# Moving a layer norm's statistics behind the projections of the group before it, in an eight-core attention and feed-forward kernel

## The reference, cut to what matters

```python
def layernorm(x):  # over the last axis, 1024 wide
    return (x - mean(x)) / sqrt(var(x) + 1e-5)

# x: (4, 4096, 1024) f32
def attention(x):              # H = 1024, one head
    y = einsum('bsh,oh->bso', x, W_qkv).reshape(*x.shape, 3)
    q, k, v = y[..., 0], y[..., 1], y[..., 2]
    attn = softmax(einsum('bqh,bkh->bqk', q, k) / sqrt(1024))
    return einsum('bsh,oh->bso', einsum('bqk,bkh->bqh', attn, v), W_out)

def ffn(x):                    # F = 4096
    # router: 8 experts, top 2, the two weights normalised, then summed
    return (gelu(x @ w1 + b1) @ w2 + b2) * combine_sum

x = x + layernorm(attention(layernorm(x)))
x = x + layernorm(ffn(layernorm(x)))
```

## Time and profile before

| | |
|---|---|
| the two timed runs | 1795.23 and 1933.11 us; their median 1864.17 us |
| the profiled execution's own time | 1799.36 us |
| its span on the slowest core (core 0) | 1797.8 us |
| spans of all eight cores | 1783.2 to 1797.8 us |
| busy share of the span: TensorE, VectorE, ScalarE, GpSimd | 80%, 29%, 32%, 10% |

### The profile page before, as it was taken

How to read it: one execution, slowest core, us unless ns; L and a number is a source line. 1 busy time by engine, 2 the same in 40 slices (tenths; PEclk the granted TensorE clock), 3 DMA queues, 4 the chain that set the end, 5 groups by cost and what they waited for, 6 DMA issues and landing times.

```text
span 1797.8 us, 19351 instructions; the slowest of 8 cores (1783.2 to 1797.8 us)
## 1 busy us (share of the span) xinstructions
PE 1439.1 (80%) x6686; PEld 652.7 (36%) x6816; DVE 523.4 (29%) x1038; ACT 574.8 (32%) x1197; POOL 170.8 (10%) x149
## 2 busy tenths in 40 slices
PE   0477787778788888888888888864998898898896
PEld 0233333333344344444443333322343343343342
DVE  0443443554233333333333333322201201202100
ACT  0412111221022333333333333344354354354334
POOL 1000000000000000000000000112013013012003
PEclk9989999998988888888888888886899899999898
DMA  9312012110220101110110000869603003002002
GB/s 140 66 30 47 27 24 44 24 24 1 35 53 7 30 30 30 30 30 30 30 30 30 30 30 30 115 131 166 103 24 94 1 24 84 11 18 77 1 1 83
DMA packets 51617, 81.55 MB, mean 45 GB/s; under 512 B 19648, under 2 KB 27840, under 8 KB 51520
## 3 DMA queue, kind: packets, MB, share of 16 engines
q0 software_dynamic: 27280, 50.35, 16.6%
q1 hardware_dynamic: 24240, 29.94, 5.3%
HBM read 97.08 MB, written 20.97 MB: 66 GB/s over the span
## 4 chain that ended last, share of the span: by engine, by line
PE 70%; DVE 11%; issue 8%; DMA 5%; ACT 4%; POOL 1%; DVEq 0%; ACTq 0%; POOLq 0%; SPq 0%
PE pAll L185 36%; PE pAll L160 31%; DMA xgb<-xo 3%; PE pAll L216 3%; DVE ptb L751 2%; DMA qs<-qstage 2%; DVE vt L497 2%; DVE xfg L440 2%; DVE m L678 1%; DVE sm L375 1%; ACT diagb L731 1%; DVE qstage L468 1%; ACT pbuf L689 1%; DMA x2lt<-x2s 1%; PE pAll L1062 1%
## 5 line engine op out<-in xcount | busy, mean ns | idle before, releaser
L160 PE MATMUL pAll<-kf,qtile 128*128 128x512 bf16 x1000 | 252.1, 407 | 16.9 <-ACT pbuf L689 9.7
L160 PE MATMUL pAll<-x2f,w1b 128*128 128x512 bf16 x1002 | 240.6, 402 | 22.7 <-ACT h1g L1163 17.0
L185 PE MATMUL pAll<-vt,ptb 128*128 128x512 bf16 x1000 | 223.7, 382 | 2.4 <-DVE ptb L751 0.9
L185 PE MATMUL pAll<-w2b,h1g 128*128 128x512 bf16 x1002 | 220.2, 379 | 5.6 <-ACT h1g L1163 4.6
L678 DVE TENSOR_REDUCE m<-pAll 128x1 f32<-128x512 f32 x128 | 88.5, 692 | 330.2 <-PE pAll L160 328.8
L689 ACT ACTIVATE pbuf<-pAll,nb 128x512 bf16<-128x512 f32 x128 | 87.3, 683 | 241.3 <-DVE nb L683 241.3
L160 PEld LDWEIGHTS pAll<-kf,qtile 128*128 128x128 bf16 x1024 | 105.7, 105 | 154.3 <-issue 56.2
L160 PEld LDWEIGHTS pAll<-x2f,w1b 128*128 128x128 bf16 x1024 | 103.9, 102 | 157.1 <-issue 55.2
L185 PEld LDWEIGHTS pAll<-vt,ptb 128*128 128x128 bf16 x1024 | 100.8, 99 | 123.7 <-issue 4.7
L185 PEld LDWEIGHTS pAll<-w2b,h1g 128*128 128x128 bf16 x1024 | 99.9, 98 | 125.9 <-issue 6.0
L185 PE MATMUL pAll<-wvb,xfg 128*128 128x512 bf16 x504 | 115.2, 379 | 35.9 <-DVE vt L497 35.5
(11 more groups left out here) (109 smaller groups left out, 1094.6 us busy)
## 6 DMA issues: line engine op xcount, KB each, us to landing
xrt<-xo POOLq DMA_DIRECT2D x16, 512.0 KB, 6.3
x2s<-x2t SPq DMA_DIRECT2D x16, 512.0 KB, 3.3
w1b<-w POOLq DMA_DIRECT2D x8, 1024.0 KB, 32.8
w2b<-w POOLq DMA_DIRECT2D x4, 2048.0 KB, 43.6
x2rt<-x2s SPq DMA_DIRECT2D x16, 512.0 KB, 4.4
y<-yt SPq DMA_DIRECT2D x16, 512.0 KB, 2.9
xgb<-xo POOLq DMA_DIRECT2D x16, 256.0 KB, 7.4
qs<-qstage POOLq DMA_DIRECT2D x16, 256.0 KB, 2.8
```

The costliest lines, as they stand in the source:

```text
L160: return e.matmul(o(), l(), r(), start=st, stop=sp)
L185: return e.matmul(o(), l(), r(), start=st, stop=sp)
```

## The change: the loads stay ahead of the projections, the statistics go behind them

`emit_ln_group` is cut in two. `emit_ln_loads(g)` issues the four loads and is called where `emit_ln_group(g)` was. `emit_ln_stats(g)` holds everything else (sums, squares, the small instructions and the application to `xng`) and is called after the projections of group g-1, just ahead of the transposes of group g. No instruction is added or taken away.

```diff
-    def emit_ln_group(g):
-        p4 = (g % 2) * 4
-        fence_s, fence_v = ln4_war[g % 2]
+    ln_dma = {}
+
+    def emit_ln_loads(g):
         src_x = xo if g < NQG else xr
         base = g * 512 if g < NQG else (g - NQG) * 512
-        ev_red = None
-        ev_sq = sqa_prev[0]
+        evs = []
         for t in range(4):
             row = base + t * 128
             dst = xgb[:, t * H:(t + 1) * H]
             w = list(last_xgb_readers.get(g - 1, []))
-            ev_dma = E.op("gpsimd", lambda e, r=row, s=src_x, d=dst:
-                          e.dma_start(d, s[r:r + 128, :]), waits=w, inc="dGp")
+            evs.append(E.op("gpsimd", lambda e, r=row, s=src_x, d=dst:
+                            e.dma_start(d, s[r:r + 128, :]), waits=w,
+                            inc="dGp"))
+        ln_dma[g] = evs
+
+    def emit_ln_stats(g):
+        p4 = (g % 2) * 4
+        fence_s, fence_v = ln4_war[g % 2]
+        ev_red = None
+        ev_sq = sqa_prev[0]
+        for t in range(4):
+            ev_dma = ln_dma[g][t]
+            dst = xgb[:, t * H:(t + 1) * H]
             wv = [ev_dma] + ([fence_v] if fence_v and t == 0 else [])
...
     for g in range(NKG):
-        emit_ln_group(g)
+        emit_ln_loads(g)
         if g >= 1:
             emit_proj(g - 1)
             ev_proj_g[g - 1] = E.ev("tS")
+        emit_ln_stats(g)
         emit_transp_group(g)
     emit_proj(NKG - 1)
```

## The result

The changed kernel takes 1858.69 us (median of 11 runs) and is slower: the ratio to the kernel before is 1.034, with a 95% interval of 1.031 to 1.037. The forecast was 1856 us and +3.2%, in a range from 1841 to 1872. In some executions of either kernel one half of the cores is granted a lower clock and the time is up to 10% longer; the ratios in this document leave these out, and the first median of the kernel before, 1864.17, was of two runs of which one, 1933.11, was such. The others of the kernel before lie close to the level from which the prediction reckoned, 1799.4: five of its ten runs took 1795 to 1798 us. Beside the median of 1864.17 alone, the forecast of 1856 would read as a little faster, which the changed kernel is not.

What follows compares the result with a forecast made beforehand. TensorE was taken to bound stage A, having work at all times but for waits. On 1799.4 us, 64.0 lost at the meetings - 3.6 - 5.1 - 0.5 + 2.0 = 56.8 us gave 1856 us, range 1841 to 1872.

Steps and rivals of the forecast that it cites:

- I add nothing: TensorE's clock at the meetings: projections already start at the lower clock, so the long idle time costs no second fall.
- the k term: k projections without q: they gain what TensorE waited for copies to `kf`, 0.5 us in all.
- rival (a): q projections of three groups: loads and stores collide in earnest and the clock falls again, 18 us, 1872 us; chance 0.15.
- 2.0 us for loads and stores that meet: First q store of groups 1 to 3: delayed by loads now issued earlier, 0.7 us each, 2 us in all.
- The gain of 1.2 us a projection: q of groups 1 to 3: VectorE is free earlier, the first store leaves 1.2 us sooner, 3.6 us in all.
- transposes: Transposes at the seven meetings: 6.8 us as in group 0 instead of 7.2, giving back 0.35 us each.
- the wait at a meeting: Last v copy to next transposes: the statistics chain is exposed, transposes start 9.5 us later at each of seven meetings.
- projection of group 0: Start of group 0's q: VectorE no longer waits there for group 1's loads, a gain of 5.1 us.
- The price of a cold start: Projections after the idle gap: by the skill's rule alone 14 us for seven; left out as paid already.
- (b): Starts of projections: removing the statistics gives back nearly what they cost at the end, net 13 us, 1813 us; chance 0.04.
- (c): Stages B and C: the rest of the kernel takes the loss back through the clock, 1799 us or less; chance 0.02.
- (d): Order of the statistics: ScalarE's or VectorE's part is still early, so the change does not do what it says; no chance given.

Runs made afterwards that it cites:

- e7_loads_behind_q: The changed kernel with the next group's four loads issued behind the q stores instead of ahead of the q copies; stage A ended at 539.4 us, no ratio.
- e1_sums_first: The changed kernel with VectorE's four sums and ScalarE's squares back ahead of the projections; 1831.89 us, ratio 1.019 to the kernel before.

## What held of the prediction, and which of its steps failed

The step on which it stood was that the statistics were hidden at the start of a projection and exposed at its end. That is what the trace shows, and the wait, by far the largest term, had the right size. The sum of the terms, 56.8 us, is also the measured sum of the phases, 56.8, but that is luck. Two steps failed and a third term was too large, and their errors cancel: 3.4 us more were gained in q of groups 1 to 3 than forecast, 1.7 less in k and 1.8 less in the transposes.

- **Failed: "I add nothing" for the clock, and with it the k term.** Forecast 0.5 us gained in k; measured 1.2 lost. The sum took the clock at the start of each projection only and had no term for k behind q. The long idle time itself did no harm: the k phases of groups 4 to 7, which follow it directly, took 63.5 us instead of 64.3, and the clock was low in them for 4.3 us each, as before (4.4). The loss is in the k phases that follow a q. In the kernel before the clock fell to 0.50 around the start of 15 of these 32, in the changed kernel of 26. Such a phase takes 15.1 to 16.7 us, one at the full clock 13.8, and groups 0 to 3 together took 60.7 us instead of 58.6. The rows show one of each: k of group 2 on core 0 before, from 220.1 us, and k of group 1 on core 1 after, from 156.78 us.

```profile
217.00:222.00 5.00, 2.23 (x11) 0.90 (x10) 1.29 (x2) 0.00 (x0) 0.85 (x3) 1.00 0.14 52
222.00:227.00 5.00, 5.00 (x25) 2.23 (x23) 2.07 (x3) 0.04 (x1) 1.89 (x4) 1.00 0.95 145
```

```profile
157.00:158.00 1.00, 1.00 (x5) 0.36 (x4) 0.24 (x1) 0.00 (x0) 0.17 (x1) 0.65 0.00 0
158.00:161.00 3.00, 3.00 (x9) 1.10 (x8) 0.69 (x1) 0.00 (x0) 0.37 (x1) 0.55 0.23 87
```

  The prediction had this fall only inside rival (a), as a consequence of colliding stores; it came without them. Why it came more often after the change stays open. TensorE's wait for the last q copy does not decide it: ahead of the first of these two k phases it was 2.77 us, ahead of the second 2.79.
- **Failed: 2.0 us for loads and stores that meet.** Forecast for q of groups 1 to 3 was 3.6 us gained less these 2.0; measured 5.0 gained (1.9, 1.3, 1.8), and `e7_loads_behind_q` finds at most 0.1 us for the meeting. The gain of 1.2 us a projection was sound: the second copy came 5.75 instead of 6.99 us after the start, and a typical q phase fell from 21.4 to 20.3 us. The rest of the 5.0 is that two pairs of cores had slow stores in the kernel before (24 to 25 us for q of one group) and none in the changed one. The slow step of the earlier trace rows, which the prediction read as a sign of what loads might do, was one of these.
- **Too large: transposes.** Forecast 0.35 us shorter each, 2.4 in all; measured 0.6 in all. The length before was taken from core 0 alone; the mean over eight cores was nearer to 6.9 than to 7.2.
- **Held: the wait at a meeting.** Forecast 9.5 us later each, 66.5 in all; measured waits of 9.6 to 9.75, 66.4 more than before in all. The chain from the v copy's end over the sums and the root to the first application holds link by link, and `e1_sums_first` took one link out and got its length back.
- **Held: projection of group 0.** Forecast 5.1 us gained; measured 25.9 to 20.7, 5.2.
- **The price of a cold start.** The Trainium skill's rule on idle gaps, "TensorE: Matmul & The Clock Gate", section on HAM oscillation, says that an idle gap like these 9.6 us makes the next work start cold. The trace agrees that it starts cold, and filling was worth 15 to 18 us, near the 14 us that the prediction worked out for the starts; but it was paid before the change as well, which the prediction read from the earlier trace rows. One figure beside it was misread: 0.32 us for a matmul of group 0 is no low rate but a mean of both, since the clock rose 4.0 us after that projection's start.
- **Rivals.** (a) would have needed 1.7 us at the first store; it was at most 0.1. Only its fall of the clock came, at 2 us a core instead of 4.5. (b) would have needed a gain of over 4 us a meeting; it was 1.3 us on average (10.2 less 1.2 over seven). (c) needed another length of the later stages; it was 1306 to 1316 us against 1306 to 1315. (d) is excluded by VectorE's timeline.

What was not tried is the wait at the meetings with another engine for the sums; and why pairs of cores have slow stores in some groups of some runs is left open.

## What to carry to other kernels

An engine that serves two masters in one queue should do the work that is not yet wanted where the waiting side has something in store. TensorE had three banks ahead of it at the start of a projection, so 6.7 us of statistics in front of the copies cost it little: 5.2 us in the first projection, where the sums waited for loads, and 1 to 2 us in each of the next three. At the end it had nothing, and the same 6.7 us cost their full length seven times, with the 2.9 us of the chain around them. Before moving a block "off the start", read in the waits how much the start really waits for it (here 0.5 us in the k groups), and look for a place inside the loop with room: one sum among two copies was hidden altogether.

## What the runs showed of the hardware that I had not expected

Eight 512-column matmuls on constants, one behind each batch of transposes, 1.7 us of work by their spacing of 0.22 us, kept TensorE at the full clock through 6.5 us of transposes that were limited by VectorE's copies, and saved 15 to 18 us of 1797 over seven meetings. They delayed nothing, since the transposes became shorter too (6.5 instead of 6.9 us). Once the clock stayed up and no store was waited for, q, k and v each took 13.8 to 14.0 us in every group from the second on.

A faster start can also bring on a collision that the slower kernel escapes: with the clock up, the first q store left at 5.0 instead of 7.0 us and met loads that landed at about 8, and the step behind it took 5.0 to 6.3 us instead of 4.3.
